# Self-attention with queries and keys projected transposed and regrouped by on-chip transfers

## What is computed

```python
x = L0_xattn(x, ctx)                          # A0, F0
x = L1_xattn(x, ctx, mask, weights)           # A1: scores * weights, masked, softmax
x = L2_xattn(ctx, ctx, x, mask)               # A2, F2
# A3
q, k, v = split(rms_norm(x) @ to_qkv)         # 16 heads x 64
q, k = q * cos + rh(q) * sin, k * cos + rh(k) * sin   # rh: (-odd, even) of each feature pair
probs = softmax(mask(q @ concat(memory, persist, k).T * 64 ** -0.5))
x = x + probs @ concat(memory, persist, v) @ to_out
x = x + silu(g) * a @ ff_w2                   # F3: a, g = split(rms_norm(x) @ ff_w1 + b)
```

## Time and profile before

| | |
|---|---|
| median of 3 runs | 2749.97 us (2748.81 to 2752.29) |
| profiled execution | 2745.54 us |
| its span, first to last instruction | 2743.7 us |
| granted TensorE clock, mean | 0.983 |
| PE (TensorE matmul) busy | 2500.9 us, 91% |
| DVE (VectorE) busy | 1876.2 us, 68% |
| ACT (ScalarE) busy | 1588.2 us, 58% |
| POOL (GpSimd) busy | 1596.7 us, 58% |
| stages, about | A0 to 427, F0 to 549, A1 to 1020, A2 to 1435, F2 to 1570, A3 to 2590, F3 to the end |

### The profile page before, as it was taken

How to read it: one execution, slowest core, us unless ns; L and a number is a source line. 1 busy time by engine, 2 the same in 40 slices (tenths; PEclk the granted TensorE clock), 3 DMA queues, 4 the chain that set the end, 5 groups by cost and what they waited for, 6 DMA issues and landing times. The chain is left out here.

```text
span 2743.7 us, 82027 instructions
## 1 busy us (share of the span) xinstructions
PE 2500.9 (91%) x26108; PEld 1758.8 (64%) x26108; DVE 1876.2 (68%) x4255; ACT 1588.2 (58%) x3469; POOL 1596.7 (58%) x2566
## 2 busy tenths in 40 slices
PE   7999999967777778999989899999999999999899
PEld 4666667955565556777768755555555555555587
DVE  5666661178888865777765667777777777777566
ACT  4777775556666655777764445555555555555433
POOL 2555553168888873555666755555555555555432
PEclk9999999989999998999999999999999999999999
DMA  4111112254544421221112200000000000000021
GB/s 116 38 38 38 38 36 60 66 152 146 149 142 143 149 84 37 46 46 46 46 41 68 63 12 15 12 15 12 14 13 12 15 12 14 13 12 14 18 59 54
DMA packets 229771, 144.42 MB, mean 53 GB/s; under 512 B 58864, under 2 KB 220657, under 8 KB 229489
## 3 DMA queue, kind: packets, MB, share of 16 engines
q1 hardware_dynamic: 229680, 143.27, 18.8%
HBM read 113.29 MB, written 29.88 MB: 52 GB/s over the span
## 5 line engine op out<-in xcount | busy, mean ns | idle before, releaser
L1632 POOL TENSOR_TENSOR sb_region<-sb_region 128x512 f32<-128x512 f32 x256 | 326.8, 1277 | 421.4 <-DVE sb_region L1559 420.0
L658 PE MATMUL bank<-sb_ident,sb_region 128*77 128x128 f32 x3072 | 414.4, 278 | 83.4 <-ACT sb_pT L746 83.4
L746 ACT ACTIVATE sb_pT<-bank 77x1024 f32<-77x1024 f32 x384 | 390.3, 1016 | 105.2 <-PE bank L658 105.2
L658 PEld LDWEIGHTS bank<-sb_ident,sb_region 128*77 128x77 f32 x3072 | 351.1, 151 | 136.9 <-issue 135.6
L842 DVE TENSOR_REDUCE sb_max<-bank 128x8 f32<-128x616 f32 x256 | 203.5, 795 | 207.1 <-PE bank L640 116.4
L1497 ACT ACTIVATE sb_region<-bank 128x512 f32<-128x512 f32 x256 | 153.0, 598 | 268.3 <-PE bank L1404 268.3
L741 ACT ACTIVATE sb_region<-sb_region 128x616 f32<-128x616 f32 x384 | 275.1, 716 | 8.5 <-POOL sb_region L979 6.2
L1404 PE MATMUL bank<-sb_wvo,sb_region 128*64 128x512 f32 x1024 | 275.6, 617 | 0.7 <-ACT sb_region L1497 0.7
L674 PE MATMUL bank<-sb_pT,sb_v 77*32 77x128 f32 x6144 | 247.8, 279 | 23.8 <-DVE sb_t L911 19.8
L1352 PE MATMUL bank<-sb_wqkv,sb_region 128*128 128x512 f32 x512 | 264.2, 599 | 0.4 <-ACT sb_region L1522 0.4
L674 PEld LDWEIGHTS bank<-sb_pT,sb_v 77*32 77x32 f32 x6144 | 145.7, 109 | 141.1 <-issue 92.3
(11 more groups left out here) (178 smaller groups left out, 5809.4 us busy)
## 6 DMA issues: line engine op xcount, KB each, us to landing
sb_region<-in_side SPq DMA_DIRECT2D x64, 616.0 KB, 3.8
scratch_after_A<-sb_y SPq DMA_DIRECT2D x256, 64.0 KB, 1.7
sb_fx<-scratch_after_A SPq DMA_DIRECT2D x96, 128.0 KB, 2.1
sb_mask<-in_mask SPq DMA_DIRECT2D x64, 154.0 KB, 2.3
sb_x<-scratch_after_F SPq DMA_DIRECT2D x128, 64.0 KB, 1.8
sb_ctx<-in_ctxT SPq DMA_DIRECT2D x192, 38.5 KB, 1.9
sb_x<-in_x SPq DMA_DIRECT2D x64, 64.0 KB, 1.8
sb_xr<-in_x SPq DMA_DIRECT2D x64, 64.0 KB, 1.8
```

What stands on the lines that cost most here:

```text
L658: mm = nc.tensor.transpose(two[0:C, h * T:(h + 1) * T], p_s[b.par][:, head * C:(head + 1) * C], ident[:])
L746: nc.scalar.activation(pT_s[k][:], two[0:C, :], ACT.Copy).then_inc(pT_kept.sem(b), 1)
L1632: nc.gpsimd.tensor_tensor(turned[what][h][:], ropeC[what][h][:], ropeS[what][h][:], ALU.add).then_inc(added.sem(b), 1)
```

## The change

In A3 the projections are made the other way round: a block of 128 columns of `wqkv` is the stationary operand and the transposed x the moving one, so q and k come out with features on the partitions and tokens along the row. Columns of `wqkv` are permuted by `scale_weights` so that even features of four heads lie in one block and odd ones in another (`eo` 0 and 1), and the rotation is then two products with transposed tables (`cosT`, `sinT`) per bank, and GpSimd's subtraction and addition across even and odd. The transposes `turn` and the copies `keep_q`, `keep_k` go away. In their place SP issues eight transfers for q and eight for k in each batch, from SBUF to SBUF, that put the features of a head on neighbouring partitions (`qF`, `kF`, double buffered); 128 packets of 512 bytes for each of q, 256 packets of 256 bytes for each of k. Both are projected two batches ahead of their scores instead of one, q in the first half of a step and k in the second; both use the same two banks. `values` gets a bank for each of its two groups, and `attend_persistent` comes behind `attend_local`. All engines' loops of A3 reach three batches ahead.

In A1 `block_keys` moves from GpSimd to ScalarE, four activations with a scale and a bias by partition straight from PSUM, without `keep_k`. VectorE's order becomes `keep_v`, `sums`, `mask`, `statistics`, `peak_masked`. The store of `vomem` is issued at the start of A2 in two parts from another buffer, and only F2 waits for it. The memory keys are projected in 32 smaller products, two tables are transposed ahead of A2, and there are four more small loads.

```diff
...
+        qF = pT_full
...
+        kF = slots("kF", [128, H * KEYS])
...
+            def block_keys(b):
+                act.wait_ge(k_made.sem(b), k_made.count(ph, b))
+                wait_earlier(act, s_made, ph, b, 2)
+                for h in range(QH):
+                    ins = nc.scalar.activation(kblk_s[b.par][:, h * C:(h + 1) * C], k_col_bank[:, K_COL:K_COL + C], ACT.Identity,
+                                               bias=key_bias_rows[:, h:h + 1], scale=rowmask[:, h:h + 1])
+                ins.then_inc(kblk_made.sem(b), 1)
...
-                    keep_k(b + 2)
+                    block_keys(b + 2) if weighted else keep_k(b + 2)
...
-                    mask(b + 1, 1)
+                    keep_v(b + 1)
                 if has(-2):
                     sums(b + -2)
                 if has(1):
-                    peak_masked(b + 1, 1)
+                    mask(b + 1, 1)
                 if has(-2):
                     statistics(b + -2)
                 if has(1):
-                    keep_v(b + 1)
+                    peak_masked(b + 1, 1)
...
-                        block_keys(b + 2)
...
+        rope_bank = bank[0:2]
+        p_bank, x_bank = bank[2], bank[2]
+        vo_banks = (bank[6], bank[3])
+        out3_bank = bank[7]
...
+            def gather(b, what, eo):
+                done = q3_turned if what == "q" else k3_turned
+                sp.wait_ge(done.sem(b), done.count(ph3, b, eo))
+                src = turned[what][eo].rearrange("p (n t) -> p n t", t=T)
+                for h in range(4):
+                    rows = slice(h % 2 * KH + eo * F, h % 2 * KH + (eo + 1) * F)
+                    if what == "q":
+                        dst = qF[b.par][rows, :].rearrange("p (n c t) -> p n c t", c=2, t=T)[:, :, h // 2]
+                        sp.dma_start(dst, src[h * F:(h + 1) * F]).then_inc(qF_loaded.sem(b), 16)
+                    else:
+                        dst = kF[b.par][rows, :].rearrange("p (c n k) -> p c n k", c=2, k=KEYS)[:, h // 2, :, 0:SEG]
+                        sp.dma_start(dst, turned[what][eo].rearrange("p (n k) -> p n k", k=SEG)[h * F:(h + 1) * F]).then_inc(kF_loaded.sem(b), 16)
...
             def step(b, has):
-                if has(3):
-                    sp.dma_start(x_s[n.par][:], tokens(source[ph3], n)).then_inc(x3_loaded.sem(n), 16)
                 if has(1):
-                    sp.dma_start(vom_s[n.par][0:H, :], at(vomem_dram, n).rearrange("b (h d) -> (b h) d", d=D)).then_inc(vom_loaded.sem(n), 16)
-                    sp.dma_start(xb_s[n.par][:], tokens(source[ph3], n)).then_inc(xr_loaded.sem(n), 16)
+                    gather_both(b + 1, "k")
+                if has(4):
+                    load_x(b + 4)
+                if has(1):
+                    load_vom(b + 1)
+                    load_residual(b + 1)
                 if has(-1):
                     sp.wait_ge(out3_taken.sem(b + -1), out3_taken.count(ph3, b + -1, 1))
                     sp.dma_start(tokens(target[ph3], b + -1), y_s[(b + -1).par][:]).then_inc(y3_stored.sem(b + -1), 16)
+                if has(2):
+                    gather_both(b + 2, "q")
...
+            def project(b, what):
+                if what == "q":
                     pe.wait_ge(xnT_kept.sem(b), xnT_kept.count(ph3, b))
-                old, old_h = half_before(b, h)
-                if old.exists:
-                    pe.wait_ge(roped[what].sem(old), roped[what].count(ph3, old, old_h))
-                nc.tensor.matmul(IN[what][:], xnT_s[b.par][:], wqkv[:, col:col + HALF], start=True, stop=True).then_inc(made[what].sem(b), 1)
-            def turn(b, what, h, more):
-                src_done, dst_done = (q3_turned, qT3_made) if what == "q" else (k3_turned, kT3_made)
-                pe.wait_ge(src_done.sem(b), src_done.count(ph3, b, h))
-                old, old_h = half_before(b, h)
-                if what == "q" and old.exists:
-                    pe.wait_ge(qT3_kept.sem(old), qT3_kept.count(ph3, old, old_h))
-                if what == "q" and h == 1 and more:
-                    pe.wait_ge(xnT_kept.sem(b + 1), xnT_kept.count(ph3, b + 1))
-                older, older_h = half_before(*half_before(old, old_h))
-                if what == "k" and older.exists:
-                    pe.wait_ge(pT3_kept.sem(older), pT3_kept.count(ph3, older, older_h))
-                dst = q_turn if what == "q" else k_turn
-                for c in range(HC):
-                    mm = nc.tensor.transpose(dst[:, c * T:(c + 1) * T], turned[what][h][:, c * 128:(c + 1) * 128], ident[:])
-                mm.then_inc(dst_done.sem(b), 1)
+                old, old_what = (b, "q") if what == "k" else (b + -1, "k")
+                for eo in range(2):
+                    if old.exists:
+                        pe.wait_ge(roped[old_what].sem(old), roped[old_what].count(ph3, old, eo))
+                    for n in range(BLOCKS):
+                        col = QPERM[what] + (eo * BLOCKS + n) * 128
+                        mm = nc.tensor.matmul(rope_bank[eo][:, n * T:(n + 1) * T], wqkv[:, col:col + 128], xnT_s[b.lap], start=True, stop=True)
+                    mm.then_inc(made[what].sem(b), 1)
...
-                if g:
-                    pe.wait_ge(vo_kept.sem(b), vo_kept.count(ph3, b, 2 * h))
-                else:
-                    old, old_h = half_before(b, h)
-                    if old.exists:
-                        pe.wait_ge(vo_kept.sem(old), vo_kept.count(ph3, old, 2 * old_h + 1))
+                old, old_h = half_before(b, h)
+                if old.exists:
+                    pe.wait_ge(vo_kept.sem(old), vo_kept.count(ph3, old, 2 * old_h + g))
                 for r in range(2):
-                    mm = nc.tensor.matmul(vo_bank[r * SEG:(r + 1) * SEG, :], xnT_s[b.par][:, g * SEG:(g + 1) * SEG],
+                    mm = nc.tensor.matmul(vo_banks[g][r * SEG:(r + 1) * SEG, :], xnT_s[b.lap][:, g * SEG:(g + 1) * SEG],
...
-                    following = (b, 1) if h == 0 else (b + 1, 0)
-                    turning = has(0) if h == 0 else has(1)
                     leaving = has(-1) if h == 0 else has(0)
+                    old, old_h = half_before(b, h)
                     if has(0):
                         scores(b, h)
-                    if turning:
-                        turn(following[0], "k", following[1], has(1))
-                        turn(following[0], "q", following[1], has(1))
-                    if has(1):
-                        project(b + 1, "q", h)
+                    if has(2):
+                        project(b + 2, "qk"[h])
                     if leaving:
-                        old, old_h = half_before(b, h)
-                        transpose_p(old, old_h, following if turning else None)
-                    if has(1):
-                        project(b + 1, "k", h)
-                    if leaving:
-                        attend_persistent(old, old_h)
+                        transpose_p(old, old_h)
                     if has(0):
                         values(b, h, 0)
+                        values(b, h, 1)
                     if leaving:
                         attend_local(old, old_h)
-                    if has(0):
-                        values(b, h, 1)
-                    if h == 1 and has(2):
-                        transpose_x(b + 2)
-            drive(pe, NB, step, reach=2)
+                        attend_persistent(old, old_h)
+                    if h == 1 and has(3):
+                        transpose_x(b + 3)
+            drive(pe, NB, step, reach=3)
...
-                    if has(0) if h == 0 else has(1):
-                        following = (b, 1) if h == 0 else (b + 1, 0)
-                        keep_k(*following)
-                        keep_q(*following)
+                    if has(0):
+                        exps(b, h)
                     if has(-1) if h == 0 else has(0):
                         keep_p(*half_before(b, h))
                     if has(0):
-                        exps(b, h)
-                    if has(0):
                         keep_values(b, h, 0)
                         keep_values(b, h, 1)
-                    if h == 1 and has(2):
-                        keep_xT(b + 2)
-            drive(act, NB, step, reach=2)
+                    if h == 1 and has(3):
+                        keep_xT(b + 3)
+            drive(act, NB, step, reach=3)
...
+            def rope(b, what, eo):
+                done, roped, added = (q3_made, q3_roped, q3_turned) if what == "q" else (k3_made, k3_roped, k3_turned)
+                dve.wait_ge(done.sem(b), done.count(ph3, b, eo))
                 if (b + -1).exists:
-                    dve.wait_ge(added.sem(b + -1), added.count(ph3, b + -1, h))
-                src = IN[what][:]
-                nc.vector.tensor_tensor(by_half(ropeC[what][h][:], KH), by_half(src, KH),
-                                        cos[:].unsqueeze(1).to_broadcast([T, 2 * HC, KH]), ALU.mult)
```

(77 more changed lines are left out.)

202 lines of the change are left out of this document (105 added, 97 removed).

## The result

The changed kernel takes 2609.34 us (median of 4 runs, 2608.07 to 2610.43) where the kernel before takes 2749.59 beside it: ratio 0.9488, 95% interval 0.9472 to 0.9505. Forecast was 2598, range 2550 to 2660. The profiled execution spans 2606.7 us, 137.0 less than before.

| stretch, by TensorE's rows | before | after | |
|---|---|---|---|
| start to A1's first scores | 558.33 | 558.73 | +0.4 |
| to A2's first transpose (A1, memory) | 480.80 | 464.71 | -16.1 |
| to F2's first transpose (A2) | 395.03 | 391.88 | -3.2 |
| to A3's first transpose of x (F2) | 141.27 | 136.42 | -4.9 |
| to A3's first scores (filling) | 12.44 | 19.24 | +6.8 |

A forecast was written before the change was run, and what follows sets the result against it. TensorE, busy 949.0 of 950 us, was taken to bound A3, and waits on VectorE to hold up A1. 2745.5 - 119 + 3 - 33 - 4 + 1 = 2593.5, plus 4 us for the runs' median: 2598, range 2550 to 2660.

The forecast's parts named there:

- Turning, -119: A3: taking 16 transposes a batch off TensorE, which sets the pace, saves 1.86 us a batch, 119 us in all.
- Projections, +0.1 us a batch: A3: 32 short passes replace 8 long ones, 3.58 us against 3.44, costing 0.1 us a batch.
- B: A3: VectorE or a hand-over sets the pace at 14.5 us a batch instead of 13.7, total 2648; chance 0.17.
- C: A3: short projection passes cost 0.157 us each, +1.6 us a batch, total 2697; chance 0.06.
- VectorE: A3: 85% busy, 0.5 us a half of idle cover left ahead of the maxima; uncovered, each 0.1 costs 13 us.
- GpSimd: A3: four additions stay four; those for q wait for scores of two batches earlier, but nothing waits twice.
- Transfers: A3: hidden within 13.7 us a batch; SP issues for 9.7 us, a packet costs 27.3 ns.
- Rival A: A3: the SBUF-to-SBUF transfers set the pace and make it slower, 2989 us at 100 ns a packet; chance 0.05.
- Filling, +3: Start of A3: two more rotations and a landing delay the first scores by 3 us, between 0 and 8.
- A1, -33: A1: two waits fall and ScalarE's q comes last, 6.5 us a batch against 7.03 over 63 batches, saving 33 us.
- Store, -4: Start of F2: the stall behind the store of `vomem` goes, saving 4 us.
- A2's start, +1: Start of A2: smaller products and two transposes cost 1 us, from 0 to 3.

## Why the prediction was right, point by point

The size and sign came out, and so did the cause: 121.5 of 137 us were won in A3, where TensorE is never idle, and 110 of them are the price of its transposes when put back. By its own steps:

- *Turning, -119:* right in kind, some 9 too large: put back, 16 transposes cost 110 us. A3 came to -121.5 with the dropped waits of the next item, less the dearer projections.
- *Projections, +0.1 us a batch:* 32 passes take 3.78, not 3.58; against the 3.44 of before that is +0.3. The up to 0.3 of dropped waits came too (both groups of `values` take 1.76 us in a row, 0.91 + 1.00 before). Period 13.70 for 13.74. Rivals B, C fall.
- *VectorE:* the wait ahead of the maxima shrank to 0.23 us (27.0 us over 117 halves), less than the 0.5 left for it. But "each 0.1 us a half costs 13 us" is wrong: one more product of 0.68 us a half, net of what another instruction lost some 0.4, cost 1.8 us in all, since its idle time elsewhere counts too.
- *GpSimd:* its additions do wait for scores (L1418, 82.5 us over 58), and nothing is late for it.
- *Transfers:* hidden as said. SP's 9.7 us a batch are 11.8, the engines' 27.3 ns a packet are 21.4. Rival A would not have come about through the engines: SP's issue is the nearer bound, 1.9 us away.
- *Filling, +3:* mis-sized, +6.8. The landing was counted, the 16 issues in a row (10.5 us) were not.
- *A1, -33:* mis-sized by half; with the memory's stage it gave 16. The scores are preceded by `sb_qT`, as said, but at 6.8 us and not 6.5. The term that failed is the one of ScalarE: the four activations take 1.20 us up to the next instruction where the one took 0.25, 0.95 more and not 0.75, "some 0.15 us comes through at most" was 0.2, and the hand-over 0.23 for 0.14. What was not seen at all is that "GpSimd loses its product" is not free: it moves GpSimd's shift onto VectorE's mask. A1 at 6.76 to 6.82 us in four kernels of different make says how near the three engines' rings lie. In kernels whose A1 is the changed one's, the stretch with the memory's stage took 464.7 to 470.0 us, so the 16 is the upper end of 11 to 16.
- *Store, -4:* F2 is 4.9 shorter. *A2's start, +1:* with smaller products it was 1.5 us shorter (from the memory's projection, L1733 before and L1731 after, to A2's first transpose: 20.0 us before, 18.4 after).
- Left open: A2 is 3.2 us shorter and F3 1.4 longer without a change to their work. F3 took 151.3 to 154.3 us in the other kernels, none of which touches it.

The sum: 137 measured, 152 forecast. A1 is 18 short (14.6 of 33), the filling 4, F3 and the start 2; the memory's stage, A2 and A3 are better by 2.5 to 3 each, F2 by 1.

The Trainium skill has the collision (SBUF — State Buffer, Who interferes with whom): a VectorE instruction with two inputs in SBUF and a GpSimd instruction that reads SBUF exclude each other, and who issues second waits. The masks at 0.79 and 1.44 to 1.85 us agree. L1016 at 0.26 and 1.08 agrees with the first half; of the second its rows show the opposite order, by 0.24 us. Weighed beforehand, with the stretched masks and shifts in the trace of the kernel before, it would have lowered the trust in A1's term. The penalty below 512 B weighed in the prediction does not show between SBUF and SBUF: 8.8 ns for 66 B.

## What to carry to other kernels

Where one engine is busy all of the time, take work off it and price the rest only by whether it fits: transfers within SBUF, a second engine at 90%, all of that was free here or nearly so. Where three engines share a ring, no edit has a price of its own: moving 0.7 us off GpSimd cost 64 us with one order of VectorE's and nothing with the other, and one added wait of 1.4 us gained 78. Before moving work between them, look for instructions whose longest duration is well over the shortest, and see what runs beside them; a median can hide them.

## What the runs showed of the hardware

- VectorE's mask (two inputs in SBUF, 128x616) takes 0.79 us, and up to 1.85 when GpSimd's shift began first; GpSimd's one-column product takes 0.26 us, and 1.08 where a mask's row begins 0.24 us after its own and both end together.
- Packets in A3, 83 to 96% of them from SBUF to SBUF on 32 partitions: 5.6 ns + 0.048 ns a byte, between means of 66 and 331 B.
- SP needs 0.65 us to issue a transfer of 128 or 256 packets between SBUF and SBUF and, eight in a row, 1.17 us for 2048 (0.63 for the first of them), against 0.34 to 0.39 for one of rows of x.
- Four activations of 128x77 from PSUM with scale and bias by partition take 1.20 us in a row, 0.30 each.
